# A perceiver layer on one core: other banks and another evicting engine for the turned probabilities of the cross-attention, and a self-attention in f16 parts in one block

## The reference, cut to what matters

```python
# 1 cross-attention: 16 heads of 64, 512 queries against 8192 keys
q, k, v = quantise(LN(x) @ Wq + bq), quantise(ctx @ Wk + bk), quantise_columns(ctx @ Wv + bv)
p = softmax(q @ k.T); p = round(p * 255 / max(p)) * max(p) / 255      # per row
x = x + (p @ v) @ Wp + bp
# 2 causal self-attention in each of the 4 batches of 128 rows, 16 heads of 64, rope on q and k
q, k, v = rope(LN(x) @ Wq + bq), rope(LN(x) @ Wk + bk), LN(x) @ Wv + bv
x = x + (softmax(mask(q @ k.T / 8)) @ v) @ Wo + bo
# 3 feed-forward, weights in fp4 with a scale for each group of 128
x = x + rmsnorm((silu(LN(x) @ Wg) * (LN(x) @ Wu)) @ Wd)
```

## Time and profile before

| | |
|---|---|
| median of 3 runs | 2849.79 us (2849.28 to 2851.23) |
| the profiled execution | 2849.09 us, its span 2847.3 us |
| busy over the span | TensorE 91%, VectorE 64%, ScalarE 37%, GpSimd 19% |
| mean granted clock of TensorE | 0.969 of full speed |
| keys and values (with the query projection) | to about 1412 us |
| cross-attention | 1419 to about 2145 us |
| projections | to 2345 us |
| self-attention | 2346 to 2436 us |
| feed-forward | 2436 to 2847 us |

### The profile page before, as it was taken

One profiled execution on the slowest core, in us unless ns is written; L12 is line 12 of the kernel. 1 busy time (PEld: TensorE's weight loads), 2 busy tenths in 40 slices (PEclk: granted clock), 3 DMA queues, 4 the chain that ended last, 5 costly groups with the idle time before them and its releaser, 6 DMA issues. The chain is left out here.

```text
span 2847.3 us, 42128 instructions
## 1 busy us (share of the span) xinstructions
PE 2580.7 (91%) x16680; PEld 1315.8 (46%) x16680; DVE 1833.1 (64%) x2736; ACT 1041.4 (37%) x929; POOL 554.3 (19%) x206
## 2 busy tenths in 40 slices
PE   6999999999999999999967777777777999999998
PEld 3444444444444444444434444444444448544443
DVE  5855555555555555555488999999983434667673
ACT  3111111111111111111278999999992215311100
POOL 0500000000000000000055664654631280100100
PEclk9999999999999999999999999999998995899999
DMA  6233443443344344334377889788865214000000
GB/s 244 59 101 99 118 103 87 112 110 89 95 125 109 75 110 119 93 91 118 93 183 185 187 199 207 182 197 206 187 134 209 89 60 76 1 16 1 15 4 30
DMA packets 557198, 321.52 MB, mean 113 GB/s; under 512 B 401953, under 2 KB 533281, under 8 KB 552353
## 3 DMA queue, kind: packets, MB, share of 16 engines
q1 hardware_dynamic: 557088, 319.91, 44.2%
HBM read 149.95 MB, written 69.21 MB: 77 GB/s over the span
## 5 line engine op out<-in xcount | busy, mean ns | idle before, releaser
L502 PE MATMUL kv_acc<-kv_whi,kv_xthi 128*128 128x512 f16 x2048 | 777.4, 380 | 5.3 <-DVE kv_xtlo L558 5.3
L502 PE MATMUL kv_acc<-kv_wlo,kv_xthi 128*128 128x512 f16 x2048 | 777.4, 380 | 0.0
L502 PE MATMUL kv_acc<-kv_whi,kv_xtlo 128*128 128x512 f16 x2048 | 777.2, 379 | 0.0
L957 DVE TENSOR_SCALAR_CACHE_REDUCE at_sc<-at_score 128x1024 f32<-128x1024 f32 x512 | 609.7, 1220 | 26.0 <-PE at_score L838 21.6
L1055 ACT ACTIVATE at_sc<-at_sc,at_bias,at_qs 128x4096 uint16<-128x4096 f32 x128 | 484.8, 3791 | 0.9 <-DVE at_bias L969 0.9
L545 ACT ACTIVATE kv_parts<-kv_key 128x1024 f16<-128x1024 f32 x64 | 67.6, 1057 | 863.5 <-DVE kv_key L583 863.5
L502 PEld LDWEIGHTS kv_acc<-kv_whi,kv_xthi 128*128 128x128 f16 x2048 | 200.6, 98 | 247.9 <-DVE kv_xtlo L558 5.8
L502 PEld LDWEIGHTS kv_acc<-kv_whi,kv_xtlo 128*128 128x128 f16 x2048 | 200.7, 98 | 242.4 <-issue 1.4
L502 PEld LDWEIGHTS kv_acc<-kv_wlo,kv_xthi 128*128 128x128 f16 x2048 | 200.6, 98 | 241.9 <-issue 1.1
L564 DVE SCALAR_TENSOR_TENSOR kv_key<-kv_acc,kv_bias 128x512 f32<-128x512 f32 x128 | 88.5, 691 | 339.7 <-PE kv_acc L502 339.7
L853 PE MATMUL at_turn<-ident,at_sc 128*128 128x128 f16 x2048 | 150.4, 223 | 122.2 <-DVE at_probt L975 91.8
(11 more groups left out here) (203 smaller groups left out, 3125.8 us busy)
## 6 DMA issues: line engine op xcount, KB each, us to landing
kv_rows<-in_ctx SPq DMA_DIRECT2D x64, 512.0 KB, 7.9
keys_turned<-kv_kt SPq DMA_DIRECT2D x32, 1024.0 KB, 5.2
values<-kv_val SPq DMA_DIRECT2D x32, 1024.0 KB, 9.5
at_v_raw<-values SPq DMA_DIRECT2D x16, 2048.0 KB, 8.7
at_kt<-keys_turned SPq DMA_DIRECT2D x32, 512.0 KB, 5.2
x<-keys_turned SPq DMA_DIRECT2D x31, 512.0 KB, 5.1
wq_stage<-in_wkv SPq DMA_DIRECT2D x4, 2048.0 KB, 7.5
x<-in_x SPq DMA_DIRECT2D x2, 2048.0 KB, 8.2
```

What stands on the lines that cost most here:

```text
L502: last = nc.tensor.matmul(acc[c][:], a[s][:, k, :], b[:, c, k, :], start=(k == 0 and q == 0), stop=(k == KD - 1 and q == 2))
L957: nc.vector.tensor_scalar(sc[n % 2][:, c * SC:(c + 1) * SC], score[pos % 2][:], 1.0, None, ALU.mult, ALU.max, accum_out=part_max[n % 2][:, ...
```

## The change

Cross-attention: quarter 2 now uses bank 0 and quarter 3 bank 1. ScalarE evicts quarters 0, 1, 2 and VectorE quarter 3, at step 6. `finish_slot` spreads TensorE's work otherwise; the sums of quarter 3 go to step 0 of the next slot. `ORDER` and `copy` stay as they are.

```diff
-    BANK = (0, 1, 1, 0)
+    BANK = (0, 1, 0, 1)
...
-                elif k == 2:
-                    pe.wait_ge(out_v, g + 1)
-                elif k == 3:
-                    pe.wait_ge(out_s, OUT0 + 3 * g + 1)
+                elif k == 1 and g:
+                    pe.wait_ge(out_v, g)
+                elif k > 1:
+                    pe.wait_ge(out_s, OUT0 + 3 * g + k - 1)
...
                 if c == 0:
                     turns(g, m, 0)
+                    if g:
+                        sums(g - 1, (m - 1) % SLOTS, 3)
+                elif c == 1:
                     turns(g, m, 1)
                 elif c == 2:
-                    turns(g, m, 2)
-                elif c == 3:
                     dma_sums(ii, g, m, 0)
                 elif c == 4:
-                    turns(g, m, 3)
+                    turns(g, m, 2)
                 elif c == 5:
                     sums(g, m, 0)
                     sums(g, m, 1)
                 elif c == 6:
+                    turns(g, m, 3)
+                elif c == 7:
                     sums(g, m, 2)
-                    sums(g, m, 3)
-                elif c == 7:
                     dma_sums(ii, g, m, 1)
...
-                        if c == 1 and not (first and n == 0):
+                        if c == 6 and not (first and n == 0):
                             turned_out(i * SLOTS + n - 1)
...
-                        if done is not None and n % T == 1 and c == 0:
+                        if done is not None and n % T == 1 and c == 2:
                             output(done, j)
...
-                        for k in (0, 2, 3):
+                        for k in range(3):
                             turned_out(g - 1, k)
```

```diff
+            for n in range(3):
+                turn_rows(n)
             scores(0)
+            turn_rows(3)
             for g in range(G):
                 if g + 1 < G:
                     scores(g + 1)
+                if g + 4 < len(units):
+                    turn_rows(g + 4)
                 turns(g)
                 if g >= 1:
                     sums(g - 1)
...
             def turns(g):
-                pe.wait_ge(exps_done, HG * (g + 1))
+                pe.wait_ge(p_split, g + 1)
...
+            def split_probabilities(g):
+                pool.wait_ge(exps_done, HG * (g + 1))
+                if g >= 2:
+                    pool.wait_ge(p_turned, g - 1)
+                hi, lo = p_parts[g % 2][:, 0:HG, :], p_parts[g % 2][:, HG:2 * HG, :]
+                nc.gpsimd.tensor_copy(hi, s[g % 2]).then_inc(p_hi_ready, 1)
+                pool.wait_ge(p_hi_ready, g + 1)
+                nc.gpsimd.tensor_tensor(lo, s[g % 2], hi, ALU.subtract).then_inc(p_split, 1)
+
+            for t in range(T):
+                split_values(t)
+            for g in range(G):
+                split_probabilities(g)
...
+                sp.wait_ge(y_turned, len(units))
```

Feed-forward: panel 9 is no longer split in the self-attention but here, after the fourth of the eight row splits, and the first four products change their order:

```diff
+    ORDER = [(0, 0), (1, 0), (0, 1), (1, 1)] + [(t, n) for t in range(2, T) for n in range(2)]
...
-            pe.wait_ge(panels.lo_ready, first + 2)
-            for t in range(T):
-                for n in range(2):
-                    products(t, n)
-                if t:
+            for t, n in ORDER:
+                products(t, n)
+                if n == 1 and t:
                     turn_x(2 * t - 2)
                     turn_x(2 * t - 1)
...
             for n in range(len(units)):
                 low_o(n)
+                if n == 3:
+                    panels.low(dve, first + 1)
             make(0)
             dve.wait_ge(row_added, 1)
-            for t in range(T):
-                take_x(t, 0)
-                take_x(t, 1)
-                normalise(t)
+            for t, n in ORDER:
+                take_x(t, n)
+                if n == 1:
+                    normalise(t)
...
             for n in range(len(units)):
                 high_o(n)
+                if n == 3:
+                    panels.high(act, first + 1)
```

More of the change, by code:

```diff
@@ L288, in _ @@
                 panels.high(act, m)
+            if after is not None:
+                after[1](act)
         @block.vector
@@ L308, in _ @@
                     panels.low(dve, m)
+                if after is not None and n == after[0]:
+                    after[2](dve)
             dve.wait_ge(panels.taken, T * (first + count))
@@ L937, in _ @@
                 finish_slot(PAIRS, 0, c)
+            sums(HEADS * T - 1, SLOTS - 1, 3)
         @block.vector
@@ L1171, in _, with turn_rows @@
         def _(pe):
+            def turn_rows(n):
+                t, h, q = units[n]
+                if n >= 2:
+                    pe.wait_ge(lo_ready, n - 1)
+                for k in range(4):
+                    at = (4 * h + k) * P
+                    last = nc.tensor.transpose(y_bank[n % 2][:, k, :], (y_q, y_k)[q][:, t, at:at + P], ident32[:])
+                last.then_inc(y_turned, 1)
             def scores(g):
                 t, c = groups[g]
+                pe.wait_ge(lo_ready, 4 * t + 2 * (c // 2) + 2)
                 if g >= 2:
                     pe.wait_ge(masked, g - 1)
+                rows, tok = slice(HD * (c % 2), HD * (c % 2) + HD), slice(t * P, (t + 1) * P)
                 for j in range(HG):
-                    h = head_of(c, j)
-                    rows, tok = slice(HD * (h % 2), HD * (h % 2) + HD), slice(t * P, (t + 1) * P)
-                    last = nc.tensor.matmul(score[g % 2][:, j, :], q_t[rows, h // 2, tok], k_t[rows, h // 2, tok],
-                                            start=True, stop=True)
+                    at = head_of(c, j) // 2
+                    for n, (a, b) in enumerate(((0, 0), (0, 1), (1, 0))):
+                        last = nc.tensor.matmul(score[g % 2][:, j, :], q_parts[a][rows, at, tok], k_parts[b][rows, at, tok],
+                                                start=(n == 0), stop=(n == 2))
                 last.then_inc(scored, 1)
             def turns(g):
-                pe.wait_ge(exps_done, HG * (g + 1))
+                pe.wait_ge(p_split, g + 1)
                 if g >= 2:
-                    pe.wait_ge(p_out, g - 1)
-                for j in range(HG):
-                    last = nc.tensor.transpose(turn[g % 2][:, j, :], s[g % 2][:, j, :], ident32[:])
+                    pe.wait_ge(p_out[g % 2], g // 2)
+                for n in range(2 * HG):
+                    last = nc.tensor.transpose(turn[g % 2][:, n, :], p_parts[g % 2][:, n, :], ident16[:])
                 last.then_inc(p_turned, 1)
@@ L1227, in outputs @@
                 dve.wait_ge(inv_ready, g + 1)
-                nc.vector.tensor_tensor(
-                    o[:, t, :].rearrange("p (c h e d) -> p c h e d", h=HG, e=2, d=HD)[:, c // 2, :, c % 2, :],
-                    outp[g % 2][:, :, 0:HD], inv[g % 2][:].unsqueeze(2).to_broadcast((P, HG, HD)),
-                    ALU.mult).then_inc(o_ready, 1)
+                nc.vector.scalar_tensor_tensor(
+                    out=o[:, t, :].rearrange("p (c h e d) -> p c h e d", h=HG, e=2, d=HD)[:, c // 2, :, c % 2, :],
+                    in0=outp[g % 2][:, :, 0:HD], scalar=1.0 / PART,
+                    in1=inv[g % 2][:].unsqueeze(2).to_broadcast((P, HG, HD)),
+                    op0=ALU.mult, op1=ALU.mult).then_inc(o_ready, 1)
+            for n in range(3):
+                low_rows(n)
             masks(0)
+            low_rows(3)
             for g in range(G):
-                if g == G // 2:
-                    panels.low(dve, split)
                 if g + 1 < G:
                     masks(g + 1)
+                if g + 4 < len(units):
+                    low_rows(g + 4)
+                if g % 2:
+                    turned_out(g)
                 if g >= 1:
@@ L1257, in turned_out, with _, split_values @@
                     act.wait_ge(summed, g - 1)
-                nc.scalar.activation(p_t[g % 2][:], turn[g % 2][:], ACT.Copy).then_inc(p_out, 1)
+                nc.scalar.activation(p_t[g % 2].bitcast(U16), turn[g % 2][:].bitcast(U16), ACT.Copy).then_inc(p_out[0], 1)
+            for n in range(4):
+                high_rows(n)
             exps(0)
             for g in range(G):
+                if g + 4 < len(units):
+                    high_rows(g + 4)
                 if g + 1 < G:
                     exps(g + 1)
-                turned_out(g)
-                if g == G // 4:
-                    panels.high(act, split)
+                if g % 2 == 0:
+                    turned_out(g)
+        @block.gpsimd
+        def _(pool):
+            def split_values(t):
+                half = slice(HALF, D)
+                nc.gpsimd.tensor_scalar(y_v[:, t, half], y_v[:, t, half], PART, None, ALU.mult).then_inc(v_step, 1)
+                pool.wait_ge(v_step, 2 * t + 1)
+                nc.gpsimd.tensor_copy(v_parts[0][:, t, half], y_v[:, t, half]).then_inc(v_step, 1)
+                pool.wait_ge(v_step, 2 * t + 2)
+                nc.gpsimd.tensor_tensor(v_parts[1][:, t, half], y_v[:, t, half], v_parts[0][:, t, half], ALU.subtract)\
```

(6 more changed lines are left out.)

141 lines of the change are left out of this document (80 added, 61 removed).

## The result

The changed kernel takes 2924.64 us (median of 4 runs, 2922.86 to 2924.87) against 2849.53 us beside it: 1.0261 times as long, 95% interval 1.0243 to 1.0279, or 75.1 us more. I had forecast 2915 and a range of 2888 to 2937. The profiled execution took 2924.87 with a span of 2923.1, and its mean granted clock is 0.962 where it was 0.969.

A forecast was written before the change was run, and what follows sets the result against it. Bounds: VectorE nearly full in the cross-attention, a closed group loop of 4.73 us in the self-attention, TensorE behind it. 2849.1 + 54 (cross-attention) + 8 (self-attention) + 4 (feed-forward's prelude) = 2915 us; range 2888 to 2937.

The forecast's parts named there:

- Cross-attention, +54: Cross-attention: the late fourth turn lengthens each slot by 0.94 us to 11.75; over 57 slots, +54 us.
- the stall of 1.2: Cross-attention, step 5: VectorE's copy of chunk 5 waits 1.2 us a slot for TensorE's fourth turn; bounds 0 and 1.24.
- The rival on the other side: Cross-attention: the fourth turn comes in time, no stall, slot falls to VectorE's 10.55 us; 2842 in all; chance 0.08.
- -15 for the cross-attention: Cross-attention without the stall: 57 slots, each 0.26 us shorter, -15 us.
- Self-attention, +8: Self-attention: GpSimd's split lengthens the group loop from 4.73 to 5.61 us at half clock; stage 98 against 90.4, +8 us.
- the term of GpSimd's start: Start of the self-attention: GpSimd first splits the values, 12 operations, 10.2 us, before group 0.
- Free edits, 0: Projection: four values' splits (2.8 us of VectorE) lie in 4.49 us pauses; SP's held-back loads are covered; no cost.
- Prelude, +4: Feed-forward's prelude: the output panel's split moved there delays VectorE's normalised rows; +4 us, bounds 0 and 5.
- The stand of TensorE: Feed-forward's prelude: after its fourth product TensorE waits 4 to 5 us for the normalised rows.
- Full clock in the self-attention: Self-attention: f16 in place of f32 lifts TensorE to full clock; -8 us, 2907 in all; chance 0.20.
- the half clock in the cross-attention, +170: Cross-attention: longer slots drop TensorE to half clock, slot some 14 us; +170, about 3025 in all; chance 0.04.
- GpSimd dearer: Self-attention: GpSimd shares access with VectorE's splits, or its copy costs as the subtraction; +12 us, 2927; chance 0.08.

The follow-up runs named there:

- e1: Kernel before with only the cross-attention's part of the change: 2903.83 us, 1.019 times the kernel before.
- e3: Cross-attention's part alone, with TensorE's fourth turn in step 5 in place of step 6: 2833.84 us, 0.9942 of the kernel before.
- e6: Self-attention's part alone, with two of GpSimd's four values' splits put behind the probabilities of groups 1 and 2: 2864.62 us, 1.005 of the kernel before.
- e12: Self-attention's part alone, without GpSimd's last additions of the keys' rotation (output lacks them): 2866.33 us, 1.0057 of the kernel before.
- e7: Self-attention's part alone, with the second output panel split in the self-attention as before, not in the prelude: 2869.00 us, 1.0064 of the kernel before.
- e5: Self-attention's part alone, with four buffers for the sums of the exponentials in place of two: 2843.93 us, 0.9978 of the kernel before.
- e2: Kernel before with all of the change except the cross-attention's lines (the self-attention's part alone): 2869.45 us, 1.0067 of the kernel before.
- e8: Self-attention's part alone, with the subtraction for the probabilities' low parts on VectorE in place of GpSimd: 2877.18 us, 1.0095 of the kernel before.

## Why the prediction was right, and where it was short

It was right in its sign, in its main term and in the mechanism of it; 2915 is 9.6 us below the measured time, inside the range.

- **Cross-attention, +54.** Measured 54.3 over the same 57 slots, 11.76 each where I had 11.75. The walk through TensorE's queue was right link by link, but for the last: from the turn's end to VectorE's start it is 0.15 us and not 0.02 to 0.06, and the stall of 1.2 is 1.26. VectorE's own work was put too high by about as much or more: it is busy 88% of 11.76, so 10.4 us and not 10.55. That the sum comes within 0.01 is luck; that it is the stall that decides is not. e1 shows that this half makes it alone, e3 that the turn's place makes it: with the turn one step earlier the stall and the 54 us are gone. One thing I had not priced: some slots in the middle last 12.0 to 12.4 us. In one of them the granted clock is 0.57 from 1912.4 to 1916.4, behind TensorE's wait of 1.44 us; why it falls there and not elsewhere stays open.
- **The rival on the other side** (no stall, 2842) did not come, but its -15 for the cross-attention did: e3, nearly without the stall, took 2834, with a slot of 10.57 us. So the change of the cross-attention (banks, evicting engine and order together; no run parts them) is good for 16 to 18 us; only the step of the fourth turn spoilt it. But a slot without the stall is not VectorE's alone: my 10.4 us for ScalarE, which "doesn't decide", are as full as VectorE's there.
- **Self-attention, +8.** Measured 11.2. The loop (5.59 against 5.61), the half clock, the copy of 0.61 and the subtraction of 1.15 were right. The step that failed is the term of GpSimd's start: I had put "4 x 2.56 = 10.2 us", with the scaling in place as cheap as a copy, and it takes 1.49 us. That is 3.6 us, and e6 gets 4.8 back by moving two of the splits.
- **Free edits, 0.** The splits of the values in the projection were to "lie in pauses of 4.49 us". They would have, at 2.8 us. Beside GpSimd's additions they took 10.33, and 1.7 us came out at the end of the stage. This is the step that was wrong in kind: I had looked at whether VectorE was free, not at what ran beside it. e12 shows it. SP's loads of words and scales, held back to the last row turn, made no wait that the trace shows.
- **Prelude, +4.** Measured 7.2. The stand of TensorE is 4.23 us as forecast; 2.4 are the lower clock behind it, left out of the sum though TensorE at half clock behind a wait stands there; VectorE's split of the panel took 5.32 beside GpSimd's addition of the bias in place of 4.42. e7, which moves the split back, is rid of all of it.
- **Full clock in the self-attention** (0.20) did not come either: 0.52. e5 shows that the same f16 work can be granted 1.00, in a shorter loop. What I had put for it was also a slip: with 0.45 and 0.55 the loop adds up to 4.92 us, not 5.03. And the half clock in the cross-attention, +170, is +182 by its own 14 us a slot. Neither moves the forecast. **GpSimd dearer** was half right: not the copy, but its neighbours on VectorE.

So both halves lost by the same kind of step. One traded a wait of 0.39 us on ScalarE for one of 1.26 on VectorE, the engine with the least air. The other unloaded TensorE in a stage whose chain was already the longer of the two, and lengthened the chain.

## What to carry to other kernels

When a step is moved in an in-order queue, walk from it to whoever reuses the buffer that it frees: here one turn behind one pair of scores cost 54 us, and one step earlier it cost nothing. When a loop over groups runs at the sum of its links, look for the smallest buffer that closes it before making the links faster: 4 x 128x4 sums in place of 2 brought 25.5 us (about a third of it by the higher granted clock that came with them) where moving the work to a faster engine lost 7.7. And before an instruction of VectorE is counted as cheap, look at what GpSimd does beside it.

## What the runs showed of the hardware that I had not expected

- VectorE's operations of 128x512 from two sources in SBUF went from 0.69 us each to 2.6 beside GpSimd's f32 additions (10.33 against 2.50 for four, e12), and one of 128x4 from 170 to 964 ns beside GpSimd's subtraction (e2 against e8). VectorE's maximum over 128x512 kept its 0.69 us inside the same subtraction (e5, 12 times).
- GpSimd scales 128x512 f32 in place in 1.49 us, and copies as many to f16 in 0.61.
- The same f16 work was granted 0.52 in the loop of 5.59 us and 1.00 in e5's of 3.62. In e5 the clock rose at about 2370.5, after TensorE had worked from 2365.9 on without a pause, and stayed up to about 2408 though TensorE waited for GpSimd in every group (busy 23.77 of 37.50 us). It then fell to 0.50, some 4 us behind the last of the row turns. What decides between the two was not settled.
